# A DLRM tower with bilinear field interaction: two doubles transposed per visit, ScalarE's accumulations placed by a rule, dense features joined with the sums

## The chip, the core and the metric

The kernel runs on one core of a Trainium2 chip. The metric is the device time of one execution in microseconds (us); less is better. The engines of the core are TensorE (PE; its weight loads are listed apart as PEld), VectorE (DVE), ScalarE (ACT), GpSimd (POOL) and SyncE (SP). They run their own instruction lists and meet at semaphores.

## What is computed

For each of 2048 samples, 32 embedding rows of 64 numbers are gathered from 32 tables. Each of the 496 pairs of fields gives one number, `p^T K q`, with a 64 x 64 kernel of its own. A linear layer and an MLP with 16 dense features follow.

```python
e = jnp.stack([tbl_f[ids[:, f]] for f in range(32)], axis=1)   # shortened
...
rows, cols = np.triu_indices(num_fields, k=1)
p = feat_emb[:, rows, :]
q = feat_emb[:, cols, :]
pij = jnp.einsum('bpe,dpe,bpd->bp', p, kernel, q)
return pij @ W.T + b
...
h = jnp.concatenate([z, dense_ctx], axis=1)
h = jnp.maximum(h @ W_top1 + b_top1, 0.0)
h = jnp.maximum(h @ W_top2 + b_top2, 0.0)
y = h @ W_top3
```

All data is fp32.

## The kernel before

The batch is worked in four groups of 512 samples (`CHUNKS`), here called groups 0 to 3. Two fields side by side make a **double** (128 numbers); there are 16 doubles, 0 to 15.

- **Gathers** (POOL, L355 to L368): for each double 8 indirect DMAs, one for each field and tile of 128 samples. Group `i`'s gather of double `j` writes over the same double of group `i - 1`, so it waits until that one has been transposed: `pool.wait_ge(s_turned, TURN_USE[i - 1, j] + 1)`. Doubles 0 to 3 have two buffers (`emb_first`); they wait for group `i - 2`'s transposes and for its last batch product. POOL does little else.
- **Turn** (PE, `turn`, L553): 4 transposes of a double into one PSUM bank. ACT copies it to `emb_t` (L403). A turn takes a place in the ring.
- **Slot** (PE, `slot`, L580): 8 small matmuls of one double against another with the pair kernels, into two PSUM banks; DVE multiplies them by `emb_t` into `prod` (L499; L494 and L496 for the two halves of a special slot). 96 slots a group.
- **Batch** (PE, L594): the same for fields 0 to 7 against rows 4 to 11, by tile; DVE multiplies (L510) and ACT sums each 64 products in a **reduce**, 8 `ACTIVATE`s with an accumulator (L444). 32 batches and 64 reduces a group.
- **Sum** (PE, L622): adds the products of two slots over partitions into `sums`. At the end of a group **join** (L606) adds the batch sums by 64 transposes; ACT copies `sums` out (L414).
- **Layer** (PE, L648): 7 steps a group, run in the next group's time at slots 10, 14, ... 34 (the last group's at the end).

Six PSUM banks form a ring of 3 places of 2 banks (`RING`, `ring_bank`); a step takes a place and PE waits in `ring_free` for whoever empties it. One list, `PROGRAM`, sets the order on PE, DVE and ACT; each engine picks its steps from it. `TURNS` and `TURNS_EARLY` tell behind which slot a turn stands; in group 0 a turn stands right ahead of its first use. The 16 dense features take 2 spare rows in each of 8 places of `sums_sb`; SP puts them there with 8 DMAs once the joined sums are copied (L342).

The trace lists each matmul of slots, batches, sums, joins and layers twice, with two weight loads: 16 records for a slot of 8 matmuls, 8 for a layer of 4.

## Time and profile before

| | us |
|---|---|
| median of 3 runs | 1359.52 (1359.11 to 1363.39) |
| the profiled execution | 1367.28 |
| its span, first to last instruction | 1365.4 |

The profile shows one execution; 1.9 us of its time lie outside the span. Its mean granted clock of TensorE is 0.83 of full speed, where 1.00 is 2.4 GHz and 0.50 is 1.2 GHz. The groups' slots start at 38.3, 550.1, 869.7 and 1145.3 us and the last slot of group 3 at 1330 us. POOL's last gather ends at 1051 us. A row of "busy times by stretch" gives, for a stretch of time, each engine's busy time with the number of its instructions in brackets.

### The profile page before, as it was taken

To read this page: it belongs to the slowest core of one execution; us is meant where nothing else is said; L and a number is where in the kernel's file an instruction comes from. 1 tells how busy PE (TensorE), PEld (TensorE's weight loads), DVE (VectorE), ACT (ScalarE), POOL (GpSimd) and SP (SyncE) were. 2 spreads that over 40 slices of the span, in tenths; PEclk is the share of its full clock that TensorE was granted. 3 is DMA by queue.
4 is the path that set the end of the run, shared out by engine and by line. 5 is a ranking of instruction groups with operands and counts; after the bars stand their busy time and mean duration, and the time that the engine had idled before them with its cause. 6 is when DMAs were issued, how large, how long until landed. Compare 5 with 4: busy or idle time off the path is not lost.

```text
span 1365.4 us, 29877 instructions
## 1 busy us (share of the span) xinstructions
PE 1075.3 (79%) x11888; PEld 350.7 (26%) x11888; DVE 615.0 (45%) x559; ACT 560.2 (41%) x4205; POOL 483.7 (35%) x517
## 2 busy tenths in 40 slices
PE   4110335779999977879999985968899999999997
PEld 2000001122334311222323320222222333333333
DVE  2000001143656622234437951334334997668990
ACT  0000000084655601024447960024425993669961
POOL 6777771544232264544442035444434000000000
PEclk9555555688998866679999995779889999999999
DMA  8111110100000010100000001000000000000000
GB/s 322 26 26 27 26 26 5 20 18 17 11 14 11 10 22 15 19 17 17 17 17 10 3 13 20 16 18 18 17 14 17 3 3 3 2 2 2 3 3 2
DMA packets 21570, 29.10 MB, mean 21 GB/s; under 512 B 11108, under 2 KB 11620, under 8 KB 20920
## 3 DMA queue, kind: packets, MB, share of 16 engines
q0 software_dynamic: 16384, 16.81, 6.3%
q1 hardware_dynamic: 3368, 8.79, 1.7%
q8 instruction: 93, 1.52, 0.5%
...
HBM read 27.17 MB, written 0.01 MB: 20 GB/s over the span
## 4 chain that ended last, share of the span: by engine, by line
PE 68%; another core or an unknown queue 14%; issue 12%; DVE 3%; ACT 2%; DMA 1%; SPq 0%; ACTq 0%; DVEq 0%
PE bilinear L580 36%; PE sums L622 16%; PE bilinear L594 8%; PE bilinear L648 6%; PE bilinear L557 2%; ACT batch_prod L444 1%; DVE prod L499 1%; DVE batch_prod L510 1%; DVE w_comb_sb L480 0%; DVE prod L494 0%; DMA b_sb<-b_top 0%; DVE prod L496 0%; PE sums L606 0%; PE bilinear L530 0%
## 5 line engine op out<-in xcount | busy, mean ns | idle before, releaser
L580 PE MATMUL bilinear<-emb_t,k_sb 64*32 64x512 f32 x6144 | 623.0, 636 | 208.9 <-issue 197.3
L499 DVE TENSOR_TENSOR prod<-bilinear,emb_t 128x1024 f32<-128x1024 f32 x352 | 419.2, 1218 | 499.3 <-remote 375.7
L444 ACT ACTIVATE batch_prod<-batch_prod 128x64 f32<-128x64 f32 x2048 | 490.1, 242 | 103.6 <-DVE batch_prod L510 98.5
L365 POOL DMA_INDIRECT emb<-table,ids_sb x384 | 362.3, 944 | 440.5 <-PE bilinear L557 329.9
L444 ACT ACTIVATION_READ_ACCUMULATOR batch_prod<-batch_prod 128x1 f32 x2048 | 386.3, 189 | 1.4 <-issue 1.3
L622 PE MATMUL sums<-prod,row_sel 64*32 64x512 f32 x2944 | 293.1, 634 | 35.0 <-issue 21.4
L580 PEld LDWEIGHTS bilinear<-emb_t,k_sb 64*32 64x32 f32 x6144 | 158.8, 111 | 575.5 <-issue 516.6
L403 ACT ACTIVATE emb_t<-bilinear 128x512 f32<-128x512 f32 x64 | 37.9, 593 | 480.5 <-PE bilinear L557 285.1
L510 DVE TENSOR_TENSOR batch_prod<-bilinear,emb_first 128x1024 f32<-128x1024 f32 x128 | 156.0, 1218 | 143.6 <-remote 112.6
L594 PE MATMUL bilinear<-k_sb,emb_t 64*32 64x512 f32 x2048 | 172.8, 622 | 2.2 <-issue 0.9
L365 POOL DMA_INDIRECT emb_first<-table,ids_sb x128 | 120.9, 945 | 126.6 <-DVE batch_prod L510 83.4
L622 PEld LDWEIGHTS sums<-prod,row_sel 64*32 64x32 f32 x2944 | 72.3, 110 | 181.4 <-issue 156.3
L594 PEld LDWEIGHTS bilinear<-k_sb,emb_t 64*32 64x32 f32 x2048 | 47.6, 111 | 78.1 <-issue 54.0
L648 PE MATMUL bilinear<-sums_sb,w_comb_sb 128*128 128x512 f32 x128 | 58.6, 603 | 3.0 <-DMA sums_sb<-dense_t 1.5
L494 DVE TENSOR_TENSOR prod<-bilinear,emb_t 64x512 f32<-64x512 f32 x32 | 22.2, 694 | 59.4 <-remote 50.8
L425 ACT ACTIVATE h_sb<-bilinear,b_comb_sb 128x512 f32<-128x512 f32 x16 | 11.0, 687 | 78.3 <-remote 49.9
L648 PE MATMUL bilinear<-h_sb,w_sb 128*128 128x512 f32 x64 | 32.9, 665 | 1.6 <-ACT h_sb L425 0.9
L648 PEld LDWEIGHTS bilinear<-sums_sb,w_comb_sb 128*128 128x128 f32 x128 | 23.2, 189 | 38.3 <-issue 34.3
L557 PEld LDWEIGHTS bilinear<-ident,emb 128*128 128x128 f32 x192 | 20.7, 143 | 45.4 <-issue 28.4
L557 PE MATMUL bilinear<-ident,emb 128*128 128x128 f32 x192 | 32.2, 292 | 0.0
L429 ACT ACTIVATE sums_sb<-bilinear,b_sb 128x512 f32<-128x512 f32 x8 | 5.5, 688 | 59.1 <-PE bilinear L648 51.9
L557 PE MATMUL bilinear<-ident,emb_first 128*128 128x128 f32 x64 | 13.0, 330 | 19.6 <-DMA emb_first<-table,ids_sb 18.0
...
## 6 DMA issues: line engine op xcount, KB each, us to landing
...
emb_first<-table,ids_sb POOLq DMA_INDIRECT x128
...
```

Of the source, the lines that this page charges most:

```text
L365: nc.gpsimd.indirect_dma_start(fields_of(i, j, t)[:, f % 2, :], None, tables[f], bass.IndirectOffsetOnAxis(ap=ids_sb[:, start + t, f:f + 1 ...
L403: nc.scalar.activation(emb_t[:, j, 0:cols(i)], bilinear[:, ring_bank("turn", i, j), 0:cols(i)], ACT.Copy).then_inc(s_emb_t, 1)
L425: nc.scalar.activation(h1_sb[:, k, 0:n], source, ACT.Relu, bias=b_comb_sb[:, k:k + 1]).then_inc(s_layer_out, 1)
L444: last = nc.scalar.activation(products, products, ACT.Copy, accum_out=batch_sums[:, t, half, row + f:row + f + 1])
L494: nc.vector.tensor_tensor(prod[EMB:P, at, 0:n], bilinear[EMB:P, bank, 0:n], emb_t[EMB:P, m - 1, 0:n], ALU.mult)
L499: last = nc.vector.tensor_tensor(prod[:, at:at + 2, 0:n], bilinear[:, bank:bank + 2, 0:n], emb_t[:, j:j + 1, 0:n].to_broadcast([P, 2, n]), ...
L510: nc.vector.tensor_tensor(batch_prod[:, use % BATCH_PRODS, :, :], bilinear[:, bank:bank + 2, :], first.to_broadcast([P, 2, COLS]), ALU.mul ...
L557: last = nc.tensor.transpose(bilinear[:, ring_bank("turn", i, j), t * P:(t + 1) * P], fields_of(i, j, t), ident[:])
L580: last = nc.tensor.matmul(bilinear[col:col + QUARTER, bank + row // EMB, 0:n], k_sb[row:row + EMB, operand, col:col + QUARTER], emb_t[row: ...
L594: last = nc.tensor.matmul(bilinear[col:col + QUARTER, bank + row // EMB, :], emb_t[row:row + EMB, m, t * P + col:t * P + col + QUARTER], k ...
L622: last = nc.tensor.matmul(sums[32 * b:32 * b + 32, half, 0:n], row_sel[rows, 31 - pos:63 - pos], prod[rows, at + b, 0:n], start=pos == 0, ...
L648: last = nc.tensor.matmul(bilinear[0:weights.shape[1], ring_bank("layer", i, k), 0:n], weights, x, start=term == 0, stop=term == LAYER_TER ...
```

## The change

Four edits:

1. Turns in groups 1 to 3 come in pairs: one step does 8 transposes into both banks of a ring place, and one `ACTIVATE` of 128 x 1024 copies them. They stand behind slots 85, 89, 93 (doubles 0 to 5, in the group before) and 2, 10, 18, 26, 34 (doubles 6 to 15). In group 0 turns stay single. POOL's wait names the step of the pair (`TURN_OF`).
2. Layers stand behind slots 12, 16, ... 36.
3. A reduce stands two units (slots or batches) behind its batch at the earliest, at most one goes in per unit, and none goes in if the next unit is followed by a turn, a layer, a join or a group's last sum (`for_scalar`). Before, all that were due went in.
4. The dense features come with one DMA per group into 16 free columns of `batch_sums`, issued once the last group's join is done. The join transposes them along with the batch sums. The batch sums' rows are packed anew, and the fold's last two copies are one instruction each.

```diff
-FIRST_LAYER = 10
+FIRST_LAYER = 12
...
-TURNS_EARLY = {83: 0, 85: 1, 87: 2, 89: 3, 91: 4, 93: 5}
-TURNS = {1: 6, 4: 7, 8: 8, 12: 9, 16: 10, 20: 11, 24: 12, 28: 13, 32: 14, 36: 15}
+TURNS_EARLY = {85: 0, 89: 2, 93: 4}
+TURNS = {2: 6, 10: 8, 18: 10, 26: 12, 34: 14}
...
+    def for_scalar(at):
+
+        return any(kind in ("turn", "layer", "join") or (kind == "sum" and (which + 1) % GROUP_QUADS == 0)
+                   for kind, i, which in behind[at])
...
-            reduces += [(at + REDUCE_LAG * (half + 1), ("reduce", i, (*which, half))) for half in range(HALVES)]
-        while reduces and reduces[0][0] <= at:
+        if kind == "batch":
+            reduces += [(at + REDUCE_LAG, ("reduce", i, (*which, half))) for half in range(HALVES)]
+        steps += behind[at]
+
+        if reduces and reduces[0][0] <= at and not for_scalar(at + 1):
             steps.append(reduces.pop(0)[1])
...
+            for i, (start, tiles) in enumerate(CHUNKS):
+
+                wait(sp, s_joined, i)
+                sp.dma_start(batch_sums[:, 0:tiles, HALVES - 1, DENSE_AT:],
+                             dense[start * P:(start + tiles) * P, :].rearrange("(t p) f -> p t f", p=P)).then_inc(s_dense, 16)
+                if i > 0:
+                    store(sp, i - 1)
+            store(sp, NCHUNKS - 1)
...
-                        pool.wait_ge(s_turned, TURN_USE[i - 1, j] + 1)
+                        pool.wait_ge(s_turned, TURN_OF[i - 1, j] + 1)
...
-                nc.scalar.activation(emb_t[:, j, 0:cols(i)], bilinear[:, ring_bank("turn", i, j), 0:cols(i)],
+                nc.scalar.activation(emb_t[:, j:j + several, 0:n], bilinear[:, bank:bank + several, 0:n],
                                      ACT.Copy).then_inc(s_emb_t, 1)
...
+                for n in range(several):
+                    pe.wait_ge(*gathered(i, j + n))
+                    for t in range(CHUNKS[i][1]):
+                        last = nc.tensor.transpose(bilinear[:, bank + n, t * P:(t + 1) * P], fields_of(i, j + n, t),
+                                                   ident[:])
...
+                pe.wait_ge(s_dense, 16 * (i + 1))
```

PE in group 1 from its slot 8 on, before. L580 are slots, L557 turns, L594 batches, L622 sums, L648 layers:

```order
L580 MATMUL bilinear<-emb_t,k_sb 32x512 x8
L557 MATMUL bilinear<-ident,emb 128x128 x4
L622 MATMUL sums<-prod,row_sel 32x512 x8
L580 MATMUL bilinear<-emb_t,k_sb 32x512 x8
L594 MATMUL bilinear<-k_sb,emb_t 32x512 x8
L580 MATMUL bilinear<-emb_t,k_sb 32x512 x8
L648 MATMUL bilinear<-sums_sb,w_comb_sb 128x512 x4
L580 MATMUL bilinear<-emb_t,k_sb 32x512 x8
L622 MATMUL sums<-prod,row_sel 32x512 x8
L580 MATMUL bilinear<-emb_t,k_sb 32x512 x8
L557 MATMUL bilinear<-ident,emb 128x128 x4
```

The same stretch in the change, from slot 10 on (L592 slots, L569 turns, L606 batches, L635 sums, L659 layers):

```order
L592 MATMUL bilinear<-emb_t,k_sb 32x512 x8
L569 MATMUL bilinear<-ident,emb 128x128 x8
L592 MATMUL bilinear<-emb_t,k_sb 32x512 x8
L635 MATMUL sums<-prod,row_sel 32x512 x8
L592 MATMUL bilinear<-emb_t,k_sb 32x512 x8
L659 MATMUL bilinear<-sums_sb,w_comb_sb 128x512 x4
L606 MATMUL bilinear<-k_sb,emb_t 32x512 x8
L592 MATMUL bilinear<-emb_t,k_sb 32x512 x8
L635 MATMUL sums<-prod,row_sel 32x512 x8
L592 MATMUL bilinear<-emb_t,k_sb 32x512 x8
L606 MATMUL bilinear<-k_sb,emb_t 32x512 x8
L635 MATMUL sums<-prod,row_sel 32x512 x8
```

Before, doubles 8 and 9 are turned four slots apart, with layer 0 between them. Now one step turns both, and the next turn stands eight slots on, with layers 0 and 1 between.

ACT in the same place, before: L444 are reduces (8 instructions each), L403 copies of a turn, L425 copies of a layer:

```order
L444 ACTIVATE batch_prod,batch_sums<-batch_prod 128x64 x16
L403 ACTIVATE emb_t<-bilinear 128x512
L444 ACTIVATE batch_prod,batch_sums<-batch_prod 128x64 x8
L425 ACTIVATE h_sb<-bilinear,b_comb_sb 128x512
L444 ACTIVATE batch_prod,batch_sums<-batch_prod 128x64 x16
L403 ACTIVATE emb_t<-bilinear 128x512
L444 ACTIVATE batch_prod,batch_sums<-batch_prod 128x64 x8
L425 ACTIVATE h_sb<-bilinear,b_comb_sb 128x512
L444 ACTIVATE batch_prod,batch_sums<-batch_prod 128x64 x16
L403 ACTIVATE emb_t<-bilinear 128x512
L444 ACTIVATE batch_prod,batch_sums<-batch_prod 128x64 x16
```

ACT in the change: L459 reduces, L418 copies of a turn, now of two banks, L440 copies of a layer:

```order
L459 ACTIVATE batch_prod,batch_sums<-batch_prod 128x64 x24
L418 ACTIVATE emb_t<-bilinear 128x1024
L459 ACTIVATE batch_prod,batch_sums<-batch_prod 128x64 x8
L440 ACTIVATE h_sb<-bilinear,b_comb_sb 128x512
L459 ACTIVATE batch_prod,batch_sums<-batch_prod 128x64 x32
L440 ACTIVATE h_sb<-bilinear,b_comb_sb 128x512
L459 ACTIVATE batch_prod,batch_sums<-batch_prod 128x64 x16
L418 ACTIVATE emb_t<-bilinear 128x1024
L459 ACTIVATE batch_prod,batch_sums<-batch_prod 128x64 x8
L440 ACTIVATE h_sb<-bilinear,b_comb_sb 128x512
L459 ACTIVATE batch_prod,batch_sums<-batch_prod 128x64 x24
```

The copies of the turns double in width and halve in number. One reduce of 8 instructions now stands between a pair's copy and layer 0's where one stood before, and the others gather behind the layers.

SP before, from the last two kernel pieces to the first store (L342 is the dense DMA, L345 the store):

```order
L332 DMA k_sb<-k_slots 128x1792
L332 DMA k_sb<-k_slots 128x2176
L342 DMA sums_sb<-dense_t 2x512 x8
L345 DMA out<-h_sb 1x512
L342 DMA sums_sb<-dense_t 2x512 x8
L345 DMA out<-h_sb 1x512
```

SP in the change (L356 the dense DMA, L338 the store):

```order
L347 DMA k_sb<-k_slots 128x1792
L347 DMA k_sb<-k_slots 128x2176
L356 DMA batch_sums<-dense 128x4x16 x2
L338 DMA out<-h_sb 1x512
L356 DMA batch_sums<-dense 128x4x16
L338 DMA out<-h_sb 1x512
```

Eight DMAs behind the copied sums have become one ahead of the join; the DMA of group 1 goes out before group 0's store.

## Rows read from the trace of the kernel before

**Rows 1.** The page, part 1: busy time of each engine over the whole span.
```profile
PE 1075.3 (79%) x11888; PEld 350.7 (26%) x11888; DVE 615.0 (45%) x559; ACT 560.2 (41%) x4205; POOL 483.7 (35%) x517
```

**Rows 2.** Stretches: length, busy PE, PEld, DVE, ACT, POOL (count), clock, DMA share, GB/s.
```profile
483.08:538.06 54.98, 35.50 (x209) 7.80 (x208) 10.26 (x9) 6.20 (x36) 30.19 (x32) 0.63 0.11 20
801.25:857.56 56.31, 36.03 (x216) 8.13 (x208) 10.50 (x9) 6.88 (x42) 30.19 (x32) 0.67 0.10 19
1125.37:1138.75 13.38, 13.37 (x216) 4.88 (x208) 10.41 (x9) 6.88 (x42) 0.00 (x0) 1.00 0.01 1
538.06:600.87 62.81, 51.66 (x424) 14.68 (x416) 17.80 (x19) 7.40 (x38) 30.18 (x32) 0.67 0.09 18
857.56:918.62 61.06, 47.72 (x424) 13.87 (x416) 17.61 (x19) 7.40 (x38) 30.19 (x32) 0.75 0.10 19
1138.75:1162.33 23.58, 23.39 (x424) 9.30 (x416) 17.62 (x19) 7.41 (x38) 0.00 (x0) 1.00 0.02 4
600.87:716.44 115.57, 106.62 (x920) 31.78 (x912) 47.69 (x42) 50.33 (x365) 52.86 (x56) 0.96 0.09 17
918.62:1040.52 121.90, 111.34 (x920) 33.85 (x912) 47.60 (x42) 50.23 (x365) 52.84 (x56) 0.90 0.08 16
1162.33:1237.72 75.39, 75.17 (x913) 25.55 (x912) 46.38 (x42) 49.47 (x359) 0.00 (x0) 1.00 0.01 2
716.44:742.44 26.00, 24.35 (x348) 8.62 (x348) 17.82 (x18) 17.84 (x144) 7.54 (x8) 1.00 0.06 12
1040.52:1066.52 26.00, 24.21 (x348) 8.62 (x348) 17.79 (x18) 17.70 (x143) 7.56 (x8) 1.00 0.06 12
1237.72:1263.72 26.00, 25.96 (x480) 9.21 (x480) 25.22 (x24) 25.11 (x206) 0.00 (x0) 1.00 0.01 3
```

**Rows 3.** Timeline of POOL, first and last gather of doubles 4 and 5, group 1.
```profile
538.99 0.94 POOL L365 DMA_INDIRECT emb<-table,ids_sb  x1 [16.20 <-PE bilinear L557]
...
557.72 0.94 POOL L365 DMA_INDIRECT emb<-table,ids_sb  x1 [0.30 <-issue]
```

**Rows 4.** Matmuls in stretches of 5 us: a burst of 16 gathers, then one of 8.
```profile
538.99:543.99 5.00, 5.00 (x82) 1.00 0.10 20
543.99:548.99 5.00, 3.93 (x21) 1.00 0.13 26
548.99:553.99 5.00, 4.37 (x9) 0.60 0.15 26
553.99:558.99 5.00, 4.08 (x6) 0.50 0.13 26
558.99:563.99 5.00, 4.66 (x31) 0.50 0.05 10
717.50:722.50 5.00, 4.91 (x71) 1.00 0.12 23
722.50:727.50 5.00, 4.28 (x17) 1.00 0.13 26
727.50:732.50 5.00, 4.20 (x73) 1.00 0.04 7
```

**Rows 5.** Timeline of PE in group 3: sum, slot, turn, batch (start, length, count).
```profile
1171.03 1.06 PE L622 MATMUL sums<-prod,row_sel 64*32 64x512 f32 x16
1171.89 1.07 PE L580 MATMUL bilinear<-emb_t,k_sb 64*32 64x512 f32 x16
1172.89 0.66 PE L557 MATMUL bilinear<-ident,emb 128*128 128x128 f32 x4
1173.47 1.09 PE L594 MATMUL bilinear<-k_sb,emb_t 64*32 64x512 f32 x16
```

**Rows 6.** Waits of the weight loads: engine, line, releaser, us in total, times, longest.
```profile
PEld sums L622 <- ACT sums_sb L414: 15.5, 7, 6.8
...
PEld bilinear L580 <- ACT emb_t L403: 3.3, 5, 0.8
```

**Rows 7.** Timeline of PE at the end: the first layers of the last group.
```profile
1340.26 4.99 PE L648 MATMUL bilinear<-sums_sb,w_comb_sb 128*128 128x512 f32 x11 [1.46 <-DMA sums_sb<-dense_t]
```

More of the change, by code:

```diff
@@ L81 @@
 BATCHED_AT = NQUADS - (NGROUPS - 1) * GROUP_QUADS
-BATCHED_ROWS = BATCHED // (HALVES * 4)
-SPARE_AT = BATCHED_AT + BATCHED_ROWS
-SPARE = 32 - SPARE_AT
-assert HALVES * 4 * SPARE == DENSE and BATCHED_ROWS % BATCHED_FIELDS == 0
+DENSE_AT = P - DENSE
+BATCHED_ROWS = [(half, 32 * b + pos) for half in range(HALVES) for b in range(4) for pos in range(BATCHED_AT, 32)][:BATCHED]
+assert BATCHED_ROWS[-1] == (HALVES - 1, DENSE_AT - 1)
 NSUMS = NGROUPS * HALVES
@@ L140, in sum_rows @@
         for c in range(2):
-            half, row = batched_row(m, c)
-            for r in range(BATCHED_FIELDS):
-                rows[(NSUMS - HALVES + half) * P + row + r] = pair_index(r, 2 * m + c)
+            for f in range(BATCHED_FIELDS):
+                half, row = batched_row(m, c, f)
+                rows[(NSUMS - HALVES + half) * P + row] = pair_index(f, 2 * m + c)
     return rows
@@ L181, in program @@
 def program():
+    behind = [[] for _ in range(len(ALL_UNITS) + SUM_LAG + 2)]
+    for at, (kind, i, which) in enumerate(ALL_UNITS):
+        if kind != "slot":
+            continue
+        if i > 0 and which in TURNS:
+            behind[at].append(("turn", i, (TURNS[which], 2)))
+        if i + 1 < NCHUNKS and which in TURNS_EARLY:
+            behind[at].append(("turn", i + 1, (TURNS_EARLY[which], 2)))
+        k = (which - FIRST_LAYER) // LAYER_EVERY
+        if i > 0 and (which - FIRST_LAYER) % LAYER_EVERY == 0 and 0 <= k < NOUTS:
+            behind[at].append(("layer", i - 1, k))
+        behind[at + SUM_LAG] += [("sum", i, q) for q in range(NQUADS) if last_slot_of_quad(q) == which]
+        if which == NSLOTS - 1:
+            behind[at + SUM_LAG + 1].append(("join", i, 0))
+    def for_scalar(at):
+        return any(kind in ("turn", "layer", "join") or (kind == "sum" and (which + 1) % GROUP_QUADS == 0)
+                   for kind, i, which in behind[at])
     steps = [("fold", 0, 0)]
     turned = 0
-    sums, reduces = [], []
+    reduces = []
     for at, (kind, i, which) in enumerate(ALL_UNITS):
@@ L188, in program @@
             needed = max(row_of(unit) for unit in ALL_UNITS[at:at + TURNED_BEFORE] if unit[1] == 0)
-            steps += [("turn", 0, j) for j in range(turned, needed + 1)]
+            steps += [("turn", 0, (j, 1)) for j in range(turned, needed + 1)]
             turned = max(turned, needed + 1)
         steps.append((kind, i, which))
-        if kind == "slot":
-            quads = [q for q in range(NQUADS) if last_slot_of_quad(q) == which]
-            sums += [(at + SUM_LAG, ("sum", i, q)) for q in quads]
-            if which == NSLOTS - 1:
-                sums.append((at + SUM_LAG + 1, ("join", i, 0)))
-            if i > 0 and which in TURNS:
-                steps.append(("turn", i, TURNS[which]))
-            if i + 1 < NCHUNKS and which in TURNS_EARLY:
-                steps.append(("turn", i + 1, TURNS_EARLY[which]))
-            k = (which - FIRST_LAYER) // LAYER_EVERY
-            if i > 0 and (which - FIRST_LAYER) % LAYER_EVERY == 0 and 0 <= k < NOUTS:
-                steps.append(("layer", i - 1, k))
-        else:
-            reduces += [(at + REDUCE_LAG * (half + 1), ("reduce", i, (*which, half))) for half in range(HALVES)]
-        while reduces and reduces[0][0] <= at:
+        if kind == "batch":
+            reduces += [(at + REDUCE_LAG, ("reduce", i, (*which, half))) for half in range(HALVES)]
+        steps += behind[at]
+        if reduces and reduces[0][0] <= at and not for_scalar(at + 1):
             steps.append(reduces.pop(0)[1])
-        while sums and sums[0][0] <= at:
-            steps.append(sums.pop(0)[1])
-    steps += [step for at, step in reduces] + [step for at, step in sums]
+    steps += [step for _, step in reduces]
+    for late in behind[len(ALL_UNITS):]:
+        steps += late
     steps += [("layer", NCHUNKS - 1, k) for k in range(NOUTS)]
@@ L551, in ring_free, with turn @@
                     pe.wait_ge(s_layer_out, i * NOUTS + which + 1)
[L553 to L558 removed]
+            def turn(i, j, several):
+                ring_free("turn", i, (j, several))
+                bank = ring_bank("turn", i, (j, several))
+                for n in range(several):
[3 more added lines that the diff above has]
+                                                   ident[:])
                 last.then_inc(s_turned, 1)
@@ L655, in _ @@
                 elif kind == "turn":
-                    turn(i, which)
+                    turn(i, *which)
                 elif kind == "slot":
```

77 lines of the change are left out of this document (30 added, 47 removed).

## The prediction, written before the changed kernel ran

> **What bounds the kernel now.** I read the page's busy times first: PE is busy 1075 of 1365 us, DVE 615, ACT 560, POOL 484 [rows 1]. PE leads, but a fifth of the span it is idle, and its mean clock is 0.83. So the question is where it loses time. The chain of waits names "issue" and an unknown queue, that is, nothing that a semaphore explains. So I compared stretches instead: the groups run the same list of steps, and only the gathers differ. Group 1 makes gathers for group 2, group 2 for group 3, and group 3 makes none.
>
> [rows 2] cuts the groups at the starts of turns 0, 4, 8 and 15. From turn 0 to turn 4 PE needs 13.38 us without gathers (last of the three rows) and 54.98 and 56.31 us while 32 gathers run. From turn 4 to turn 8: 23.58 us without, 62.81 and 61.06 with 32 gathers. From turn 8 to turn 15: 75.39 without, 115.57 and 121.90 with 56. The matmul counts agree (up to 7 records). So gathers cost PE 41 us and more in each of these stretches, though they move little: the DMA share is about 0.1. Without them PE is busy all of its time at clock 1.00: there is no other bound behind it to relieve.
>
> The gathers' **shape** matters. POOL starts one each 1.25 us, 16 of them in 20 us [rows 3]. In the first 5 us of such a burst PE runs 82 matmuls, then 21, 9 and 6 in the next three stretches of 5, where a quiet stretch of 26 us with 480 has 92 in 5 us [rows 2, 4]. After the second of these the clock is at 0.50, and it stays there in the next 5 us with 31 matmuls. A burst of 8 (10 us) gives 71, 17, 73, with the clock at 1.00 all through [rows 4]. So a burst's first 5 us are nearly free, what lies beyond is nearly lost, and a long one takes the clock as well. Which resource they share no row shows; I argue from the price alone.
>
> **Prices of bursts**, all from [rows 2]:
> - 8 gathers, no layer near: in the 26 us from turn 15 PE runs 348 matmuls where it runs 480 without gathers; 132 x 26 / 480 = 7.2 us. (Group 2's such stretch has 348 too.)
> - 8 gathers, with a layer in nearly every burst: turn 8 to turn 15 holds 7 bursts. (115.57 - 75.39) / 7 = 5.7, (121.90 - 75.39) / 7 = 6.6. Mean 6.2.
> - 16 gathers: turn 4 to turn 8 holds two such bursts, doubles 4 and 5, 6 and 7. (62.81 - 23.58) / 2 = 19.6, (61.06 - 23.58) / 2 = 18.7. Mean 19.2.
> - 32 gathers: 54.98 - 13.38 = 41.6 and 56.31 - 13.38 = 42.9. Mean 42.3.
>
> Two bursts of 8 cost 12.4 to 14.4 us, one of 16 costs 19.2. This decides the case.
>
> **The change part by part.**
>
> *Turns in pairs, POOL's side.* POOL's wait for double j is now met for both doubles of a pair at once. In groups 1 and 2 doubles 8 to 15 stood apart, eight bursts of 8 each: (40.2 + 7.2) + (46.5 + 7.2) = 101.1 us. They become four bursts of 16 in each group. At 19.2 that is 8 x 19.2 = 153.6. But the layers now stand two slots behind each pair's turn. A layer of 8 long matmuls passes a burst better than slots do: with one a burst of 8 cost 6.2, without one 7.2, so I take 1.0 off for each: 8 x 18.2 = 145.6. The bounds: 16 (three times that credit, since a second layer could fall in as well) and 20 (above the dearer of the two groups). Term: +44.5, from +27 to +59. Doubles 4 to 7 come in two bursts of 16 already. Between their turns there is now 6.0 us of PE work (seven steps of 0.86), and a burst of 16 lets PE do about 82 + 21 + 9 + 6 = 118 matmuls, 6.3 us worth, in its 20 us [rows 4], so double 6's gathers start about where double 5's end. If they join to one of 32, a group pays 42.3 instead of 38.4. I take half of 2 x 3.9: +4, from 0 to +8. Gathers of group 1 hang on group 0's single turns and stay; doubles 0 to 3 hang on a batch product and stay; group 3 has none.
>
> *Turns in pairs, PE's side.* A visit costs 0.58 us from the turn to the next step, and the slot ahead takes 1.00 instead of 0.86 [rows 5]. A pair needs the same eight transposes; it saves the 0.14. 24 visits go in groups 1 to 3: 24 x 0.14 = 3.4 us. That it fills both banks of its place does nothing more where PE waits for no bank. A wider copy could make PE wait for the place; if each of 24 waited 0.5 us it would be 12 us, but three steps of 0.86 lie between, and the copy of 512 columns is of 0.6 us: I take 0.
>
> *Reduces kept from the copies.* PE's weight loads waited 15.5 us for the copies of the sums and 3.3 us for those of turns [rows 6]. The first lie at the joins of groups 0 and 1, inside bursts, where the copy starts late after PE's signal and not behind a reduce. I take 2 us of gain, from 0 to 19. In the quiet stretches ACT hides behind PE, which is busy 75.17 of 75.39 us [rows 2]. Of the moved layers and sums each keeps its length: 0. At most one reduce goes in per unit; 64 reduces in 128 units leave room, and each batch's last reduce still stands more than a batch ahead of the product that needs its buffer: 0.
>
> *Dense features.* 32 small DMAs and their wait go. They were on the path once, at the end: layer 0 of the last group waited 1.46 us for them [rows 7]. In the groups before they had ten slots of time. Now the join waits for a DMA issued a group earlier: 0. Gain 1.5. The fold's fewer copies lie ahead of the second turn's gather, which PE waits for anyway: 0.
>
> *Sum:* +44.5 + 4 - 3.4 - 2 - 1.5 = +41.6 on the profiled execution's 1367.3 us. Its 1.9 us outside the span stay, and it lies 7.8 us above the median; I carry the difference over: 1359.5 + 41.6, rounded to **1400 us**, 3.0% slower. With the terms' ends: 27 + 0 - 3.4 - 19 - 1.5 = +3 at the very lowest, 59 + 8 + 12 - 3.4 - 1.5 = +74 at the highest; not all at one end, 1383 to 1418.
>
> *A rule beside it.* PE's clock fell to 0.50 only in the long burst [rows 4]. The Trainium skill, "Perfetto Trace Analysis", section Matmul Optimizations, says it is important that matmuls execute back to back in batches. By it, grouped turns would help the clock; the trace has it at 1.00 over single turns in group 3, so by the rule alone the sum would lack nothing but the bursts' term.
>
> **Rivals.**
> - *Gathers cost by their number, not their grouping.* Then the 44.5 and the 4 go, and 6.9 us of gain remain: 1353 us. With more of the 19 us of waits for ACT, 1340. For it: the stretch with 16-bursts also holds the join and the group's first steps, which may be dear of themselves. Against it: the same steps take 23.58 us in group 3, and the counts by 5 us show the second half of a burst passing 15 matmuls. It decides from a price of a 16-burst below 13.0: 8p - 101.1 + 4 - 6.9 = 0. Chance 0.13. The Trainium skill, "DMA: Bandwidth & Descriptors", section SWDGE vs HWDGE vs iDMA, points this way: inside a DMA engine the queues are served in turn, so a fetch or another queue's transfer need not wait out a run of gathers. No row here shows what PE waits for.
> - *The second double hides under the layers.* A burst of 16 costs 13 to 15, if layers 0 and 1 both fall in: 8 x 14 = 112, +11 + 4 - 6.9: 1368 us, or no change at 13. Against: between them stand seven or eight steps, more than a burst lets through. Chance 0.09.
> - *Bursts run into each other.* PE is so slow behind a long burst at half the clock that the bursts of doubles 4 to 9 join and each pair costs over 20: 8 x 22 = 176, +75 + 8 - 6.9: 1436 us; from 1420. For it: 4 to 7 nearly touch. Against: from turn 6 to turn 8 stand 15 us of work, and recovery after a burst took 5 to 10 us [rows 4]. Chance 0.10.
>
> **How the numbers follow.** Forecast 0.68 (1383 to 1420), rivals 0.13, 0.09, 0.10. The range 1372 to 1422 holds the forecast's whole and a part of the second and third rival; about 0.2 is out. A measurement of this kernel can tell about 0.3% from no change, 4 us. Faster by more: 0.13. Within: 0.04. Slower: 0.83.
>
> **What would show it.** In the profile after: POOL's gathers of doubles 8 to 15 in groups 1 and 2 in runs of 16 (20 us); the stretch from the pair's turn of 8 to the 26 us behind that of 14 longer than before by some 20 us in each; group 3 shorter by 1 to 2 us; PE's issue gaps and the share of clock 0.50 up; the first layer at the end without its 1.46 us. I am wrong if a run of 16 there costs under 13 us, or if group 0, whose bursts don't change, moves by more than 5 us.

## The result, and where the time came from

| | before | after |
|---|---|---|
| median of the timed runs, us | 1359.32 (1357.87 to 1363.39, 4 runs) | 1388.92 (1386.17 to 1389.55, 4 runs) |
| the profiled execution, us | 1367.28 | 1389.55 |
| its span, us | 1365.4 | 1387.8 |
| its mean granted clock | 0.83 | 0.80 |

All of this ran on one chip, chip 1 below. The ratio is 1.0209 (95% interval 1.0183 to 1.0235): the changed kernel is 29.6 us slower. The forecast was 1400 us, with 1372 to 1422 as its range. Between the two profiled executions the difference is 22.3 us, because that of before lies above all its timed runs.

The page after, busy time of each engine, then tenths of busy time in 40 slices (compare with [rows 1]):

```profile
PE 1088.0 (78%) x11888; PEld 357.9 (26%) x11888; DVE 609.4 (44%) x553; ACT 559.9 (40%) x4181; POOL 484.9 (35%) x517
...
PEclk8555555689889967678888995767887999999999
```

PE has as many matmuls as before and is busy 12.7 us longer, at a lower clock; the rest is idle time.

POOL after, group 1: the first gather of doubles 8 and 9, and the first of doubles 10 and 11. All other gathers between them read `0.30` or `0.31 <-issue`:

```profile
605.26 0.95 POOL L380 DMA_INDIRECT emb<-table,ids_sb  x1 [16.57 <-PE bilinear L569]
...
624.01 0.95 POOL L380 DMA_INDIRECT emb<-table,ids_sb  x1 [0.30 <-issue]
...
644.40 0.95 POOL L380 DMA_INDIRECT emb<-table,ids_sb  x1 [19.45 <-PE bilinear L569]
```

The burst is one of 16 gathers, then POOL waits 19 us for the next pair's turn. The stretches of 5 us through it, columns as in [rows 4] but with all engines:

```profile
605.50:610.50 5.00, 5.00 (x54) 2.04 (x39) 1.82 (x2) 2.45 (x17) 3.78 (x5) 1.00 0.11 23
610.50:615.50 5.00, 3.46 (x19) 0.52 (x17) 0.00 (x0) 0.00 (x0) 3.78 (x5) 1.00 0.15 26
615.50:620.50 5.00, 1.84 (x13) 0.34 (x13) 1.23 (x1) 0.00 (x0) 3.78 (x5) 0.55 0.14 26
620.50:625.50 5.00, 3.95 (x11) 0.42 (x4) 0.00 (x0) 3.07 (x21) 3.54 (x4) 0.50 0.14 26
625.50:630.50 5.00, 4.23 (x28) 1.45 (x35) 2.35 (x2) 2.97 (x21) 0.00 (x0) 0.50 0.03 7
```

54 matmuls, then 19, 13 and 11, with the clock falling in the third stretch (0.55) and at 0.50 after it: the shape of [rows 4], now at the places where a burst of 8 stood.

**What the gathers cost, stretch by stretch.** The starts of turns are marks that stand at the same steps of the program in every group. So I take the time from one turn to another and subtract what the same steps take on chip 3 (below), where gathers cost PE nothing. What is left holds the waits and the low clock. The stretch from turn 8 to the next group's turn 0 holds the gathers of doubles 8 to 15, in groups 1 and 2, before and after:

```profile
600.90:801.30 200.40, 189.80 (x2349) 61.75 (x2341) 123.69 (x110) 125.18 (x973) 60.40 (x64) 0.97 0.06 12
918.60:1125.40 206.80, 194.44 (x2349) 63.85 (x2341) 123.62 (x110) 124.94 (x973) 60.40 (x64) 0.94 0.06 12
```

```profile
603.90:821.40 217.50, 199.24 (x2345) 66.72 (x2341) 122.69 (x109) 124.64 (x957) 62.03 (x66) 0.87 0.06 12
938.80:1156.10 217.30, 198.55 (x2341) 65.97 (x2341) 122.98 (x110) 124.10 (x957) 60.53 (x64) 0.86 0.06 11
```

On chip 3 these steps take 153.3 and 153.2 us in the kernel before, 151.2 and 151.3 in the changed one. Lost to gathers, in us:

| stretch | bursts | before | after |
|---|---|---|---|
| group 0, its first slot to turn 0 of group 1 | those for group 1 | 254.4 | 253.3 |
| turn 0 to turn 4, twice | doubles 0 to 3, 32 each | 41.5 + 42.9 = 84.4 | 41.2 + 41.6 = 82.8 |
| turn 4 to turn 8, twice | doubles 4 to 7 | 39.2 + 37.3 = 76.5 | 38.8 + 40.3 = 79.0 |
| turn 8 to turn 0, twice | doubles 8 to 15 | 47.06 + 53.58 = 100.6 | 66.29 + 66.05 = 132.3 |

Doubles 8 to 15 brought +31.7 us, and the other three rows together -0.2. By pairs, from one turn to the next, the eight bursts of 16 cost 17.3, 15.7, 15.9, 17.3, 17.1, 15.7, 16.1 and 17.2 us, 16.5 in the mean.

### The profile page after: what moved, and what is told of

It reads as the page before. It is cut to its first block, busy times and chain, and to the rows that moved or that the text cites. A ratio compares the mean times of both kernels' runs of the same rounds, so it can differ in the third digit from the quotient of the medians.

```text
span 1387.8 us, 29768 instructions
## 1 busy us (share of the span) xinstructions
PE 1088.0 (78%) x11888; PEld 357.9 (26%) x11888; DVE 609.4 (44%) x553; ACT 559.9 (40%) x4181; POOL 484.9 (35%) x517
## 4 chain that ended last, share of the span: by engine, by line
PE 72%; issue 16%; another core or an unknown queue 7%; ACT 3%; DVE 1%; DMA 0%; ACTq 0%; DVEq 0%
PE bilinear L592 35%; PE sums L635 15%; PE bilinear L606 11%; PE bilinear L659 6%; ACT batch_prod L459 3%; PE bilinear L569 2%; PE sums L619 1%; DVE prod L509 1%; DMA b_sb<-b_top 0%; PE bilinear L535 0%; PE bilinear L540 0%; DVE w_comb_sb L491 0%; ACT emb_t L418 0%; DVE batch_prod L520 0%
## 5 line engine op out<-in xcount | busy, mean ns | idle before, releaser
L592 PE MATMUL bilinear<-emb_t,k_sb 64*32 64x512 f32 x6144 | 611.4, 635 | 209.6 <-issue 179.7
L459 ACT ACTIVATE batch_prod<-batch_prod 128x64 f32<-128x64 f32 x2048 | 490.3, 243 | 107.0 <-DVE batch_prod L520 92.0
L459 ACT ACTIVATION_READ_ACCUMULATOR batch_prod<-batch_prod 128x1 f32 x2048 | 387.1, 189 | 9.9 <-issue 9.7
L635 PE MATMUL sums<-prod,row_sel 64*32 64x512 f32 x2944 | 296.3, 639 | 27.2 <-issue 24.6
L592 PEld LDWEIGHTS bilinear<-emb_t,k_sb 64*32 64x32 f32 x6144 | 159.4, 112 | 567.8 <-issue 496.6
L606 PE MATMUL bilinear<-k_sb,emb_t 64*32 64x512 f32 x2048 | 219.5, 650 | 10.3 <-issue 10.0
L418 ACT ACTIVATE emb_t<-bilinear 128x1024 f32<-128x1024 f32 (+1 forms) x40 | 34.0, 850 | 404.1 <-PE bilinear L569 269.1
L635 PEld LDWEIGHTS sums<-prod,row_sel 64*32 64x32 f32 x2944 | 77.7, 112 | 181.2 <-issue 165.9
L606 PEld LDWEIGHTS bilinear<-k_sb,emb_t 64*32 64x32 f32 x2048 | 52.3, 113 | 116.2 <-issue 101.4
L659 PE MATMUL bilinear<-sums_sb,w_comb_sb 128*128 128x512 f32 x128 | 58.4, 603 | 1.3 <-ACT sums_sb L429 1.3
L440 ACT ACTIVATE h_sb<-bilinear,b_comb_sb 128x512 f32<-128x512 f32 x16 | 11.0, 687 | 107.6 <-remote 54.8
L429 ACT ACTIVATE sums_sb<-sums 128x512 f32<-128x512 f32 x16 | 8.7, 594 | 81.0 <-PE sums L619 41.2
L619 PE MATMUL sums<-ident,batch_sums 128*32 128x128 f32 x256 | 19.7, 302 | 19.0 <-issue 18.6
L659 PEld LDWEIGHTS bilinear<-sums_sb,w_comb_sb 128*128 128x128 f32 x128 | 23.2, 189 | 36.0 <-issue 35.1
L504 DVE TENSOR_TENSOR prod<-bilinear,emb_t 64x512 f32<-64x512 f32 x32 | 22.2, 695 | 22.8 <-PE bilinear L592 13.4
L444 ACT ACTIVATE sums_sb<-bilinear,b_sb 128x512 f32<-128x512 f32 x8 | 5.5, 688 | 61.7 <-remote 33.6
L659 PE MATMUL bilinear<-h_sb,w_sb 128*128 128x512 f32 x64 | 29.3, 603 | 0.9 <-ACT h_sb L440 0.9
L569 PE MATMUL bilinear<-ident,emb 128*128 128x128 f32 x192 | 29.6, 297 | 0.0
```

Of the source, the lines that this page charges most:

```text
L418: nc.scalar.activation(emb_t[:, j:j + several, 0:n], bilinear[:, bank:bank + several, 0:n], ACT.Copy).then_inc(s_emb_t, 1)
L459: last = nc.scalar.activation(products, products, ACT.Copy, accum_out=batch_sums[:, t, half, row:row + 1])
L504: nc.vector.tensor_tensor(prod[EMB:P, at, 0:n], bilinear[EMB:P, bank, 0:n], emb_t[EMB:P, m - 1, 0:n], ALU.mult)
L569: last = nc.tensor.transpose(bilinear[:, bank + n, t * P:(t + 1) * P], fields_of(i, j + n, t), ident[:])
L592: last = nc.tensor.matmul(bilinear[col:col + QUARTER, bank + row // EMB, 0:n], k_sb[row:row + EMB, operand, col:col + QUARTER], emb_t[row: ...
L606: last = nc.tensor.matmul(bilinear[col:col + QUARTER, bank + row // EMB, :], emb_t[row:row + EMB, m, t * P + col:t * P + col + QUARTER], k ...
```

## Experiments

Five chips were used, numbered here in the order of the runs. In the expectations, "the first chip" to "the third chip" are chips 1 to 3, and of the three on which gathers cost, "the third of them" is chip 4. Each experiment is compared with the kernel before on its own chip. Medians in us:

| chip | before | after | others |
|---|---|---|---|
| 1 | 1359.32 | 1388.92 | |
| 2 | 1389.74 | | grouped 1417.03, split 1373.43, single turns 1372.06, paced 1242.41 |
| 3 | 851.29 | 842.19 | dense alone 850.16, reduces alone 852.85 |
| 4 | 1390.42 | 1399.63 | paced 1241.41 |
| 5 | 851.47 | | half rows 851.48 |

### Chip 2: the grouping alone

The kernel before, with POOL waiting for the odd double of each pair, so that two bursts of 8 become one of 16. PE, DVE and ACT keep their lists.

```diff
-                        pool.wait_ge(s_turned, TURN_USE[i - 1, j] + 1)
+                        pool.wait_ge(s_turned, TURN_USE[i - 1, j | 1 if i > 1 else j] + 1)
```

> The kernel before with one edit on GpSimd alone: the gathers of groups 2 and 3 for a double of 4 to 15 wait until both doubles of its pair (4 and 5, ... 14 and 15) are turned, so they go in bursts of 16. TensorE, VectorE and ScalarE keep their lists. Theory A (the price hangs on a burst's length): eight pairs of bursts of 8 become eight bursts of 16, at the 16 to 17 us each that the changed kernel shows against 101 us before: +27 to +35 us, 1387 to 1394. Rival B (gathers cost by their number): no change, 1359. Rival C (the loss comes from the turns' or reduces' new order on TensorE and ScalarE): no change either, 1359.

Measured: 1417.03 us (1412.78 to 1418.78), ratio 1.02 (1.0153 to 1.0247), +27.3 us. One wait on POOL, moved a few slots later, costs nearly what the whole change costs on chip 1 (+29.6); the changed kernel itself was not timed on chip 2. The eight bursts of 16 at doubles 8 to 15 cost 15.7 to 20.9 us each, 142.2 together (the prediction had 8 x 18.2 = 145.6 for such bursts). No trace of the kernel before was taken on chip 2.

### Chip 2: the change without its grouping

The changed kernel, with the gathers of doubles 9, 11, 13 and 15 held back by four more slots:

```diff
+                        if i > 1 and j in (9, 11, 13, 15):
+                            at = next(s for s, d in TURNS.items() if d == j - 1)
+                            pool.wait_ge(s_prod, (i - 1) * NSLOTS + at + 4 + 1)
```

> The changed kernel with one edit on GpSimd alone: the gathers of doubles 9, 11, 13, 15 for groups 2 and 3 wait besides for the product of the slot four behind their pair's turn, so doubles 8 to 15 go in bursts of 8 again. A: the loss of about 30 us goes, and what the other edits bring (3 to 7 us) is left: 1351 to 1359. B and C: it stays at 1389.

Measured: 1373.43 us (1369.83 to 1374.24), ratio 0.988 (0.9838 to 0.9923), -16.3 us. The changed kernel, with its bursts of 16, took 1399.63 us on chip 4, where the kernel before takes the same time as here (1390.42 and 1389.74). Put beside that run's trace, this one loses the same to gathers in group 0 up to turn 0 (255.7 here, 255.6 there), from turn 0 to 4 (84.0, 84.4) and from turn 4 to 8 (81.7, 81.6). From turn 8 to turn 0 it loses 110.6 where the other loses 138.7. The same gathers, turns and copies, only the bursts parted, and 28 us gone just there: so the reason stands. The size against the kernel before was not expected; more of it below.

Its bursts of 8 have **two prices**. Stretches of 5 us through the one of double 12 (price 4.3 us) and the one of double 15 (11.0 us), group 1:

```profile
680.00:685.00 5.00, 5.00 (x68) 1.65 (x52) 2.45 (x2) 4.40 (x33) 3.78 (x5) 1.00 0.11 20
685.00:690.00 5.00, 4.64 (x14) 1.32 (x14) 0.29 (x1) 0.00 (x0) 3.59 (x4) 1.00 0.14 26
690.00:695.00 5.00, 4.88 (x79) 2.33 (x83) 3.48 (x4) 3.73 (x28) 0.00 (x0) 1.00 0.05 10
731.50:736.50 5.00, 4.59 (x56) 1.10 (x41) 1.82 (x3) 4.96 (x43) 3.78 (x4) 1.00 0.10 20
736.50:741.50 5.00, 4.61 (x8) 0.44 (x6) 0.00 (x0) 0.90 (x7) 3.78 (x4) 0.57 0.15 26
741.50:746.50 5.00, 4.29 (x34) 0.98 (x41) 4.19 (x4) 0.00 (x0) 0.00 (x0) 0.50 0.04 10
746.50:751.50 5.00, 5.00 (x88) 1.43 (x80) 3.84 (x4) 3.93 (x32) 0.00 (x0) 0.91 0.01 2
```

In the first the clock stays at 1.00 and PE is back at 79 matmuls at once. In the second it falls to 0.50 and PE does 34 in the stretch behind the gathers. The eight prices of group 1 are 7.5, 6.5, 6.4, 5.1, 4.3, 4.8, 10.2 and 11.0, those of group 2 7.5, 6.2, 6.9, 5.1, 4.3, 4.8, 9.8 and 10.8: the same place in the program pays the same price twice. So here it is the place that decides what a burst costs, not chance; at some doubles of the kernel before on chip 1 the two groups differ by 2 to 3 us, though. What makes a place dear no run shows.

### Chip 2: the reduces' rule and the dense part, with single turns

The changed kernel with `TURNS`, `TURNS_EARLY` and `FIRST_LAYER` of before:

```diff
-FIRST_LAYER = 12
+FIRST_LAYER = 10
...
-TURNS_EARLY = {85: 0, 89: 2, 93: 4}
-TURNS = {2: 6, 10: 8, 18: 10, 26: 12, 34: 14}
+TURNS_EARLY = {83: 0, 85: 1, 87: 2, 89: 3, 91: 4, 93: 5}
+TURNS = {1: 6, 4: 7, 8: 8, 12: 9, 16: 10, 20: 11, 24: 12, 28: 13, 32: 14, 36: 15}
```

> The changed kernel with single turns and layers behind the slots of before; the rule for the reduces and the joined dense features stay. A: 1352 to 1358, 2 to 6 us below the kernel before (1.5 for the dense features at the end, 0 to 4 for the reduces). C, if the reduces' rule or the dense DMA costs the time: above 1365, up to 1389.

Measured: 1372.06 us (1366.99 to 1374.07), ratio 0.9868 (0.9822 to 0.9914), -17.7 us, far beyond what was expected. Its bursts of 8 at doubles 8 to 15 cost from 3.5 to 11.6 us, 105 in all. The dear ones (9.0 to 11.6 us) are at doubles 10, 12 and 15 in both groups.

### Chip 2: gathers spaced out

The changed kernel; every 4 gathers wait for three more slots of the group before.

```diff
+                        if i > 0:
+                            pool.wait_ge(s_prod, (i - 1) * NSLOTS + 3 * f + 1)
```

> The changed kernel with the gathers of groups 1 to 3 spread over the whole group before: every 4 gathers (one field) wait besides for the product of slot 3 x field. 96 bursts of 4 (5 us) at most instead of bursts of 8, 16 and 32. A, if the first 5 us of a burst are nearly free as the 5 us counts say (82 of 92 matmuls): 1 to 3 us for each of the 96 instead of about 340 us for all, so 1389 - 340 + 96 to 288: 1145 to 1337. If the backlog outlives a gap of 5 us and adds up: 1360 to 1420. B (by number): 1389.

Measured: 1242.41 us (1229.29 to 1244.63), ratio 0.8956 (0.8919 to 0.8993), -147 us.

### Chip 3: the kernel before, where gathers cost nothing

> The kernel before, unchanged, for its trace beside those that follow. Every theory expects a ratio of 1.00. If the chip is one on which the kernel before takes about 1390 us and not 1360, the theory that the burst's price sets the difference between chips expects the extra time in groups 0 to 2, while gathers run, and none in group 3 (185 us at the first chip, from its first slot to its last).

Measured: 851.53 us, beside 851.29 (849.36 to 852.16) for the same kernel in the other runs. On this chip the kernel takes 508 us less than on chip 1. The page's head:

```profile
span 849.7 us, 29877 instructions
...
PE 787.1 (93%) x11888; PEld 286.6 (34%) x11888; DVE 611.5 (72%) x559; ACT 557.6 (66%) x4205; POOL 483.9 (57%) x517
```

The groups, from each one's first slot to the next one's, on chip 1 and then on chip 3, both the kernel before (columns as in [rows 2]):

```profile
38.30:550.10 511.80, 318.29 (x2829) 97.83 (x2829) 151.61 (x134) 137.96 (x1046) 255.67 (x271) 0.70 0.09 18
550.10:869.70 319.60, 278.00 (x2966) 84.47 (x2966) 152.03 (x137) 139.41 (x1051) 120.76 (x128) 0.86 0.08 15
869.70:1145.30 275.60, 250.87 (x2969) 81.97 (x2975) 151.60 (x137) 139.20 (x1051) 82.10 (x87) 0.90 0.06 12
1145.30:1329.80 184.50, 184.06 (x2934) 65.74 (x2926) 148.91 (x136) 135.41 (x1045) 0.00 (x0) 1.00 0.01 3
```

```profile
38.40:248.80 210.40, 179.13 (x2831) 65.08 (x2838) 150.59 (x134) 136.32 (x1046) 158.94 (x169) 0.89 0.15 28
248.80:439.10 190.30, 189.76 (x2979) 67.56 (x2970) 150.53 (x137) 138.71 (x1051) 143.98 (x153) 1.00 0.15 29
439.10:629.60 190.50, 189.71 (x2979) 67.47 (x2971) 150.60 (x137) 138.84 (x1051) 143.88 (x154) 1.00 0.15 29
629.60:814.10 184.50, 184.06 (x2936) 65.69 (x2928) 148.95 (x136) 135.41 (x1045) 11.89 (x13) 1.00 0.02 5
```

Group 3, which makes no gathers on chip 1, takes 184.50 us on both. Groups 1 and 2 of chip 3 hold over 150 gathers each, one right behind the other, and PE is busy 189.8 of 190.3 and 189.7 of 190.5 us with the clock at 1.00. The gathers themselves are the same: 0.94 us each, one each 1.25 us, 26 to 29 GB/s while they run. The packets of their queue took 6.3% of 1365.4 us, that is 86 us, on chip 1 and 10.4% of 849.7, 88 us, on chip 3; the packets of the queue of instructions q8 0.5% and 0.8%, 6.8 us on both:

```profile
q0 software_dynamic: 16384, 16.81, 6.3%
...
q8 instruction: 93, 1.52, 0.5%
```

```profile
q0 software_dynamic: 16384, 16.81, 10.4%
...
q8 instruction: 93, 1.52, 0.8%
```

So neither bandwidth nor the length of a transfer makes the difference. Gathers keep PE from issuing on chips 1, 2 and 4 and don't on chips 3 and 5. Why is open: no row shows what PE waits for.

One guess lies near: that the gathers hold up PE's instructions on their way in. The packets of q8 speak against it. There are 93 of 16 KB on both chips, and they follow PE's program: in groups 1 to 3 one starts about every 128 matmuls (of those the trace lists). Were they late on chip 1, PE would be further on in its program when each starts than on chip 3. It isn't: the 93 places differ by at most 32 matmuls, in either direction, and 75 of them by at most 10. The 8 packets that start in a burst past its first 5 us differ by at most 17.

One thing differs in the pages beside PE: on chip 3 the gathers have a median time from issue to landing, 2.5 us, and on chip 1 none is given.

### Chip 3: the change and its small parts without the bursts' price

> The changed kernel, unchanged, timed on the same chip as its two small parts. Burst theory: +21 to +30 us against before (at the first chip +29.6; the two runs that undid or did the grouping alone gave -16.3 for the change without it and +27.3 for the grouping alone; if effects add up, about +11). A result near +11 says that the first chip's +29.6 is not the grouping alone; one near +29 that the parts do not add up.

Measured: 842.19 us (840.66 to 842.69), ratio 0.9893 (0.9874 to 0.9912), -9.1 us: where a burst costs nothing, the change is a gain. The same 5 us stretches as those on chip 1 above, from the pair's turn on (doubles 8 and 9, group 1):

```profile
272.00:277.00 5.00, 5.00 (x54) 1.99 (x42) 3.27 (x3) 2.67 (x17) 3.78 (x5) 1.00 0.14 30
277.00:282.00 5.00, 5.00 (x75) 1.62 (x82) 2.36 (x2) 3.68 (x27) 3.78 (x5) 1.00 0.15 26
282.00:287.00 5.00, 5.00 (x68) 1.79 (x53) 4.71 (x6) 4.64 (x40) 3.78 (x5) 1.00 0.14 30
287.00:292.00 5.00, 5.00 (x69) 1.67 (x67) 2.17 (x3) 3.02 (x22) 3.78 (x5) 1.00 0.14 28
```

54 matmuls in the first stretch on both chips; then 75, 68, 69 here and 19, 13, 11 there, with the gathers one each 1.25 us on both.

The dense part alone (one DMA per group, packed rows, shorter fold):

```diff
-                sp.wait_ge(s_sums_out, (i + 1) * NSUMS)
-                for b in range(8):
...
+                wait(sp, s_joined, i)
+                sp.dma_start(batch_sums[:, 0:tiles, HALVES - 1, DENSE_AT:],
```

> The kernel before with the dense features' part alone (one DMA per group ahead of the join, packed rows, shorter fold). The prediction gave it -1.5 us. The run with this, the rule for the reduces and single turns gave -17.7 us where the prediction's terms give -6.9 with the pairs' 3.4. If the dense part holds the rest, it gives -10 to -14 here; if the reduces do, -1 to -3.

Measured: 850.16 us (847.87 to 851.38), ratio 0.9986 (0.9975 to 0.9996), -1.1 us.

The rule for the reduces alone:

```diff
-            reduces += [(at + REDUCE_LAG * (half + 1), ("reduce", i, (*which, half))) for half in range(HALVES)]
-        while reduces and reduces[0][0] <= at:
+        if reduces and reduces[0][0] <= at and not for_scalar(at + 1):
```

> The kernel before with the rule for the reduces alone, turns single and layers where they were. The prediction gave it -2 us, from 0 to -19. If the reduces hold the rest of the -17.7 us, -12 to -17 here, and the waits of PE for ACT's copy of the sums (15.5 us before) shorter; if the dense part does, 0 to -5.

Measured: 852.85 us (850.62 to 854.07), ratio 1.0021 (1.0008 to 1.0033), +1.6 us. Where it loses them is not shown, since its profiled execution is one of its fastest, 850.99 us against the 851.53 of the kernel before. There it gains 0.5 to 0.7 us in each of groups 1 to 3, and group 0 is 1.3 longer: PE waits 12.6 us for copies of turns in group 0, before 5.4, and 0.7 for DVE, before 5.3. The longest two waits of PE for the copy of a turn there, before and with the rule:

```profile
108.38 1.96 PE L580 MATMUL bilinear<-emb_t,k_sb 64*32 64x512 f32 x16 [3.39 <-ACT emb_t L403]
120.31 1.46 PE L580 MATMUL bilinear<-emb_t,k_sb 64*32 64x512 f32 x16 [2.06 <-ACT emb_t L403]
```

```profile
108.36 1.96 PE L590 MATMUL bilinear<-emb_t,k_sb 64*32 64x512 f32 x16 [5.80 <-ACT emb_t L413]
120.29 1.09 PE L590 MATMUL bilinear<-emb_t,k_sb 64*32 64x512 f32 x16 [3.24 <-ACT emb_t L413]
```

`for_scalar` looks only at steps in `behind`, and group 0's turns are not entered there: they go in right ahead of their slots. So nothing keeps reduces from standing in front of just the copies that PE waits for most. That the longer waits come from this is my reading; no run parts it.

### Chip 4: once more where gathers cost

> The changed kernel once more, since chips differ: the kernel before took 1360 us on the first, 1390 on the second and 851 on the third, where gathers cost TensorE nothing. Burst theory: the ratio follows the time of the kernel before. Where that is near 851 us, -9 us; where it is near 1360 to 1390, +21 to +30 us (measured at the first chip: +29.6). The rival (the parts as the second chip measured them add up): +11 us on a chip of 1360 to 1390.

Measured: 1399.63 us (1398.67 to 1403.54) beside 1390.42 (1388.02 to 1394.91) before, ratio 1.0068 (1.0045 to 1.0092), +9.2 us. The burst theory's +21 to +30 missed; the rival, which added up chip 2's parts, was nearly right (+11). The changed kernel's groups, from slot to slot as above:

```profile
38.00:547.70 509.70, 317.00 (x2829) 95.40 (x2833) 151.38 (x134) 138.55 (x1043) 249.10 (x264) 0.69 0.09 18
547.70:887.80 340.10, 281.02 (x2977) 87.09 (x2968) 151.30 (x137) 139.15 (x1043) 120.76 (x128) 0.80 0.07 14
887.80:1184.40 296.60, 258.41 (x2977) 83.16 (x2971) 151.55 (x137) 138.06 (x1043) 88.69 (x94) 0.85 0.07 12
1184.40:1366.70 182.30, 181.95 (x2936) 66.92 (x2928) 148.67 (x136) 134.97 (x1040) 0.00 (x0) 1.00 0.01 3
```

On chip 1 they took 506.80, 333.60, 293.10 and 182.30. Its bursts at doubles 8 to 15 sum to 138.7, against 132.3 on chip 1. The changed kernel is 11 us slower here than on chip 1, and the kernel before 31 us. So the ratio differs because of the kernel *before*. Where that one loses them, the grouped run tells in part. In group 0 and at doubles 0 to 3 its bursts are those of the kernel before. There it lost 257.6 + 84.8 us on chip 2, and the kernel before 254.4 + 84.4 in the execution profiled on chip 1, 3.6 less. But the kernel before takes 22 us more on chip 2 than that execution took. With group 3 at 184.5 us on both, the rest, about 19 us, must lie mostly at doubles 4 to 15.

> The changed kernel with POOL's gathers spaced by the slots of the group before (4 gathers every 3 slots), as it ran 147 us faster than before at the second chip. If bursts are what costs, it brings 110 to 150 us again where the kernel before takes 1360 to 1390 us, and nothing beyond the change's own -9 us (from -12 to +5, since gathers may now come late) where it takes 851. If the gain came from something else that the waits do (another order of the queues, a later POOL), it shows on a chip of 851 too.

Measured: 1241.41 us (1234.17 to 1243.01), ratio 0.8915 (0.8877 to 0.8954), -149 us. Its groups, and some of its gathers in group 1:

```profile
38.30:453.00 414.70, 266.39 (x2829) 93.10 (x2836) 150.72 (x134) 137.48 (x1043) 213.88 (x227) 0.79 0.10 19
453.00:736.80 283.80, 258.71 (x2974) 97.57 (x2965) 152.72 (x137) 139.85 (x1043) 120.72 (x129) 0.96 0.09 17
736.80:1019.80 283.00, 262.10 (x2972) 94.83 (x2964) 152.32 (x137) 139.56 (x1043) 120.68 (x129) 0.96 0.09 17
1019.80:1204.70 184.90, 184.28 (x2936) 67.43 (x2928) 149.23 (x136) 134.97 (x1040) 3.13 (x4) 1.00 0.02 3
```

```profile
511.10 0.94 POOL L382 DMA_INDIRECT emb_first<-table,ids_sb  x1 [0.30 <-issue]
517.35 0.94 POOL L382 DMA_INDIRECT emb_first<-table,ids_sb  x1 [5.30 <-DVE prod L511]
...
525.97 0.94 POOL L382 DMA_INDIRECT emb_first<-table,ids_sb  x1 [3.94 <-DVE prod L511]
```

After each 4 gathers POOL waits, 4.3 us in the middle (1.1 to 11.2 in groups 1 and 2), and the clock in groups 1 and 2 is 0.96 instead of 0.80 and 0.85. Against the changed kernel on the same chip, group 0 is 95.0 us shorter, group 1 56.3, group 2 13.6, and group 3 2.6 longer. Without gathers' price groups 1 and 2 take 186.9 each (chip 3), so 258 gathers cost 96.9 + 96.1 us here, 3.0 for four (PE waits for no gather to land in these groups); in the changed kernel 222 cost 153.2 + 109.7, 4.7 for four. So four gathers cost 3.0 us spaced out, 3.5 in a burst of 8 (the split run's mean, 6.9), 4.1 in one of 16 (16.5) and 5.2 in one of 32 (41.4). The long bursts are the dear ones, but even four gathers are not free.

### Chip 5: half the bytes

The kernel before, with its gathers for groups 2 and 3 at half a row:

```diff
-                                fields_of(i, j, t)[:, f % 2, :], None, tables[f],
+                                fields_of(i, j, t)[:, f % 2, 0:EMB if i < 2 else EMB // 2], None,
+                                tables[f] if i < 2 else tables[f].rearrange("v (a e) -> (v a) e", a=2),
```

> The kernel before, unchanged, for its trace. On two chips it took 1390 us, on the first 1360, and the changed kernel 1389 at the first and 1400 at the third of them. Theory: a burst of 8 has two prices, 4 to 7 us where it passes without a fall of the clock and 9 to 11 where the clock falls (both seen in the runs with bursts of 8 at the second chip), and a slower chip has more of the dear ones. Where this run takes about 1390 us it expects the bursts of doubles 8 to 15 in groups 1 and 2, 104 us at the first chip, at 120 to 135, each with a stretch of clock 0.50, and group 0 within 5 us of 506. The rival: the 30 us lie in group 0 or in the bursts of 16 and 32 (85 and 78 us at the first chip), and the bursts of 8 stay at 104.

> The kernel before with every gather for groups 2 and 3 fetching half a row (128 bytes instead of 256; the numbers it then works with are others): as many gathers, descriptors and waits, half the bytes. If what TensorE loses goes by the bytes moved, the bursts in groups 1 and 2 cost half or less (32 gathers some 42 us before, 16 some 19 to 20) and the kernel gains 80 to 130 us where before takes 1360 to 1390. If it goes by the gathers issued, their prices stay within 10% and the time within 10 us. Where before takes 851 us, both expect no change.

Measured: 851.42 us (849.15 to 852.79) for the kernel before and 851.48 (851.09 to 852.63) with half rows, ratio 1.0003 (0.9994 to 1.0013). This chip is of the kind of chip 3, where no burst costs anything, so both runs say nothing on their questions: whether the price goes by bytes or by gathers, and at which of these bursts chips 2 and 4 lose more with the kernel before, stay open.

## Why the prediction held, step by step

**The split of the sum.** Chip 3 shows what each group takes without the bursts' price, so the time on chip 1 parts cleanly. Before: (511.8 - 210.4) + (319.6 - 190.3) + (275.6 - 190.5) + 0 = 515.8 us lost to gathers. After, with 212.3, 186.9, 186.9 and 182.3 on chip 3: 294.5 + 146.7 + 106.2 + 0 = 547.4. That is +31.6 from gathers and -9.4 from everything else (spans 849.7 and 840.3), together +22.2; the spans on chip 1 differ by +22.4. The prediction had +48.5 and -6.9. The medians differ by 29.6: the profiled execution of before lay 8 us above its median, that of after 0.6. I had carried the first difference over to the forecast. In which stretch those 8 us lie no trace shows; if in the bursts, these cost less than listed in most executions of the kernel before, and the change added more.

- **Bursts of 16 in place of 8**, taken at +44.5 (27 to 59): +31.7 by the table above. The direction and the mechanism hold, shown by the grouping alone (+27.3) and by parting the bursts again. The bursts of 8 before were priced right (101.1, and 100.6 by the table). The size missed in the price of 16: I took 18.2 and the mean was 16.5, 13 us over eight. At doubles 4 to 7 the same kernel paid 19.8 (79.0 for four), so bursts of 16 are cheaper at doubles 8 to 15, by more than the 1.0 that I took off for a layer. Whether it is the layers isn't shown, and they can't be all of it: in group 3 the pairs of 8, 10 and 12 alike have a layer of 8 matmuls 4 to 5 us behind their turn, and yet their bursts cost 17.2, 15.7 and 16.0 us in the mean. One reading of mine was off, too: before, doubles 4 to 7 came in two bursts of 16 only nearly, since POOL rested 1.5 to 1.8 us between doubles 6 and 7.
- **Doubles 4 to 7 merging to 32**, taken at +4 (0 to 8): they didn't merge (POOL rests 7 us between the two bursts). The stretch moved by +2.5, and that of doubles 0 to 3 by -1.6.
- **Group 0**, said to stay within 5 us: it is 5.0 shorter on chip 1, +1.9 that chip 3 shows too and -6.9 less lost to gathers. But its end cuts through a burst, and the next group starts inside it. Up to turn 0, ahead of that cut, the loss moved by -1.1 only, so most of the 6.9 went over the boundary. The limit was too fine for such a cut.
- **Pairs on PE's side**, taken at -3.4: about -7. I priced only the slot ahead (1.00 for 0.86) and left the eight transposes at twice 0.58. Group 3 after:

```profile
1212.48 1.06 PE L635 MATMUL sums<-prod,row_sel 64*32 64x512 f32 x16
1213.48 1.09 PE L569 MATMUL bilinear<-ident,emb 128*128 128x128 f32 x8
1214.51 1.09 PE L592 MATMUL bilinear<-emb_t,k_sb 64*32 64x512 f32 x16
1215.39 1.06 PE L606 MATMUL bilinear<-k_sb,emb_t 64*32 64x512 f32 x16
```

  From the pair's first transpose to the next step pass 1.03 us, not 1.16: a visit has its own price inside the 0.58 as well. Two visits cost 2 x (0.14 + 0.58) = 1.44 beyond the neighbours, one 0.14 + 1.03 = 1.17; that is 0.27, and 0.27 x 24 = 6.5, with what the step behind it gains about 7. This is worked out from the rows and not timed alone.
- **Reduces**, taken at -2 (0 to -19): alone +1.6, outside the range, which allowed no loss. I looked at the copies that the rule protects and not at group 0's, which it doesn't see; whether those hold the loss is open.
- **Dense features**, taken at -1.5: -1.1. The wait at the end is gone; layer 0 of the last group now waits only for the copy of the sums, `[1.30 <-ACT sums_sb L429]`.
- The parts alone (-1.1, +1.6) and the pairs (-7) give -6.5 of the -9.1. The other 2.6 I can't place; some of it is noise, since each of the three differences is known to 1 or 1.6 us.

**The rivals.** That gathers cost by their number and not by their grouping falls on chips 1 and 2: a burst of 16 at doubles 8 to 15 cost 15.7 to 17.3 us (chip 1) and 15.7 to 20.9 (chip 2), above the break-even of 13.0. The page of the Trainium skill named beside it, "DMA: Bandwidth & Descriptors", section SWDGE vs HWDGE vs iDMA, has the queues inside a DMA engine served in turn, so that another queue's transfer need not wait out a run of gathers. The trace agrees, on chip 1 as on chip 3: q8's packets come at the same places of PE's program on both. So nothing here speaks against the rule, and PE loses its time on chips 1, 2 and 4 all the same. That the second double hides under layers, 13 to 15 for a burst, came nearer than its 0.09 said: two pairs of four reached 15.7 to 16.1. That it was the layers which did it isn't shown. Bursts running into each other didn't occur: between pairs POOL rests 16.6 to 19.5 us. The sign I named as sure, the stretch from the turn of 8 to 26 us behind that of 14, was badly cut: it is 140.1 us in group 1, against 141.6 before, because between its ends lie 24 slots now and 28 before. Whole groups tell it.

**What chance had in it.** The forecast's +41 was right in sign on chip 1 (+29.6) and on chip 4 (+9.2), and wrong on chip 3 (-9.1), whose kind the profile gave no hint of. Alone or undone, the grouping is worth 27.3 (chip 2) and 26.2 (1399.63 against 1373.43, two chips with the same time before). What differs is the rest: on chip 2 the other parts bring 16.3 us with the pairs and 17.7 without them, on chip 3 all edits together 9.1. The bursts of 8, with their two prices by place, are the only term seen to vary that much: if four of sixteen fell from 10.5 to 6.5, it would be 16 us. That is an argument and not shown, since the trace of the kernel before on such a chip is missing. So the cause of the slowdown on such chips is shown, and how large it comes out on a given one is not understood.
